# A two-layer decoder in one kernel: new instruction orders for all engines and one merged queue instead of three stages

## The chip, the cores and the metric

The kernel runs on one NeuronCore of one Trainium2 chip. The metric is the device time of one execution in microseconds. Before the change it is 4436.27 us, the median of 3 runs (4430.77 to 4455.68).

## The reference, cut to what matters

Input x is (64, 64, 128), that is 4096 tokens of width 128 in float32, with a context of the same shape. Six blocks follow one another, each with a residual and, outside it, a layernorm of its input:

```
x = x + delta_rule_attention(layernorm(x))          # "A": 4 heads, sequential rule over 64 tokens
x = x + causal_attention(layernorm(x), ctx)         # "B": 16 heads of 8
x = x + ffn_block(layernorm(x))                     # "C": 6 layers, each:
    #   y = local_attention(shift(y) @ Wqkv; 16 heads of 64, l2norm, rotary, window 32) @ Wo + y
    #   y = (a * gelu(gate)) @ W2 + y, with [a, gate] = layernorm(shift(y)) @ W1; 128 -> 2*341 -> 128
x = x + clipped_attention(layernorm(x))             # "D": 16 heads of 8
x = x + gated_attention(layernorm(x), ctx)          # "E": 8 heads of 16, exp and log gates
x = x + mixture_of_experts(layernorm(x))            # "F": 16 experts, top 3, all computed
```

All arithmetic is float32.

## The kernel before, in words

The 4096 tokens are 32 tiles of 128 tokens (two sequences of 64 each). x, y (the running value of block C) and the context stay in SBUF. Work is cut into units. A unit AB is blocks A and B of one tile (32 units). A unit C1 is the attention of one layer of block C for one tile (6 x 32 = 192), a unit C2 is the feed-forward part of one layer for a group of four tiles (6 x 8 = 48). A unit DE is blocks D, E and F of one tile (32 units). Units C1 and C2 stand in one sequence, in groups of five: four C1, then the C2 of an earlier group.

Each unit is a set of named phases on four engines ("pe", "act", "dve", "pool"); a phase is one to some hundred instructions and adds 1 to a semaphore of its unit when it ends. The order is written out by hand in the strings AB_ORDER, C_ORDER and DE_ORDER (lines 78 to 113). In such a string, `p04` says: in slot n, do phase p0 of unit n-4. The digit is the lag. In C_ORDER a 1 or 2 in front names C1 or C2. Slot after slot the whole string is walked, so each engine works on several units at once, in a fixed order; an engine that waits for a semaphore holds up everything behind it in its string. `program` (line 445) runs the three stages one after the other: all slots of AB, then a prelude, then all slots of C, then all slots of DE. On every engine the first phase of C stands behind the last phase of AB, and the first of DE behind the last of C. `all_ab` (line 299) makes the first users of BIG, the banks and the small tiles wait for the last eight AB units; `all_c` (line 303) does the same for DE.

PSUM has 8 banks (`bank`). AB and DE take them in turn (8), C takes 6 in turn and keeps banks 6 and 7 for the scores. BIG is a scratch area of 25,600 floats a partition, laid out anew for each stage by `ab_bufs`, `c_bufs`, `c2_bufs`, `de_bufs`. In C the arrays T1, T2 and sq are there twice (tiles t and t-2 share one), and qT, kT, VV and P three times.

A C1 unit goes: x (transpose in), q, k, v for halves 0 and 1 (matmul 128x512), squares on ScalarE, products with rotary tables on VectorE (lines with tile rc and rs), sums on GpSimd (q, k), norm by nine small VectorE steps n0 to n8, scaling on GpSimd (n0, n1, 128x1024), transposes a and b, scores s, maximum, exponential, row sum, reciprocal, scaling on GpSimd (p), transposes p, products y and w, output projection o. Line numbers in the profile are mostly those of helpers: L557 is a matmul, L561 a transpose, L901 a copy on ScalarE, L909 another activation, L1109 tensor_tensor, L1114 tensor_scalar, L1117 scalar_tensor_tensor and L1120 reduce on VectorE, L1549 tensor_tensor and L1552 inverse root on GpSimd.

In layer 0 of block C the layernorm of x makes y. It is made by `first_norm` and `first_pow` (tile mvF), which run in the orders as the phases `first` and `second`; they have semaphores of their own (rot0, rot1, y0) and are no phases of a unit.

In a DE unit the phase G makes the scores of E and the spread gates; then VectorE makes dm and mx, GpSimd d2, ScalarE ex (exponential), VectorE C, and PE ct (four transposes). Phases h and k are first expert layers (PE h, ScalarE relu h and k), o and x the second (PE o, VectorE x). ScalarE needs the functions Exp and Ln in each DE unit (g1 Exp, g2 Ln, x3, e0, e1, ex, em Exp) and Exp and Gelu in C.

## Time and profile before

| what | us |
|---|---|
| median of 3 runs | 4436.27 |
| span of the profiled execution | 4433.1 |
| PE busy (matmul) | 4137.5 (93%) |
| VectorE busy | 3566.6 (80%) |
| ScalarE busy | 3444.4 (78%) |
| GpSimd busy | 2650.6 (60%) |

The profiled execution is the span of 4433.1 us from its first instruction to its last; the median lies 3.2 us above it. The page cuts the span into 40 slices of 111 us. Block AB takes the first five slices, C the next 26, DE the rest. Busy time is the union of an engine's instructions; the end of a matmul is modelled. The granted clock is the TensorE clock as a share of full speed, 1.00 or 0.50 at any moment.

### The profile page before, as it was taken

The numbers are of one execution on the slowest core, as the hardware profiler recorded it, in microseconds if no ns is written. First come the engines' busy times: TensorE is split into PE (matmuls) and PEld (weight loads), VectorE is DVE, ScalarE is ACT, GpSimd is POOL, SyncE is SP. The second block draws the span as 40 slices with busy tenths as digits, with TensorE's granted clock in tenths as the row PEclk, the third lists the DMA queues.
The fourth block names the chain that finished last, engine by engine and source line by source line (L and its number), as shares of the span: only waits on it lengthen the run. The fifth ranks groups of instructions, "written<-read, shape, count | busy, mean of one in ns | idle before, by whom it ended". The sixth has DMA issues, their size and how long they took to land.

```text
span 4433.1 us, 150676 instructions
## 1 busy us (share of the span) xinstructions
PE 4137.5 (93%) x61520; PEld 3049.0 (69%) x61520; DVE 3566.6 (80%) x11101; ACT 3444.4 (78%) x9647; POOL 2650.6 (60%) x2210
## 2 busy tenths in 40 slices
PE   7999989999999999999999999999999689999999
PEld 5777756666666666666666666666666478888888
DVE  4666599999889888899898989898989357766775
ACT  3555478889888888888888988888888357776776
POOL 3444377777777777777777777777777133333331
PEclk8888899999999999999999999999999789999999
DMA  3000000000000000000000000000000100000000
GB/s 101 4 4 4 4 3 4 5 3 4 29 4 4 4 28 4 4 4 13 20 3 4 5 28 4 4 4 8 7 9 9 47 2 4 4 4 4 4 4 6
DMA packets 65258, 46.43 MB, mean 10 GB/s; under 512 B 29220, under 2 KB 63032, under 8 KB 63800
## 3 DMA queue, kind: packets, MB, share of 16 engines
q1 hardware_dynamic: 64568, 36.78, 2.9%
q8 instruction: 487, 7.98, 0.7%
q14 instruction: 203, 1.66, 0.1%
HBM read 28.48 MB, written 2.10 MB: 7 GB/s over the span
## 4 chain that ended last, share of the span: by engine, by line
PE 68%; ACT 13%; DVE 10%; POOL 5%; issue 5%; SPq 0%; DVEq 0%; DMA 0%; ACTq 0%; POOLq 0%
PE ps L557 56%; PE ps L561 12%; ACT BIG L909 7%; DVE BIG L1109 5%; POOL BIG L1549 5%; ACT L909 2%; ACT BIG L901 2%; DVE sm L1120 2%; ACT ps L901 1%; DVE BIG L1117 1%; DVE BIG L1114 1%; POOL sm L1552 0%; DVE sm L1117 0%; DVE BIG L1187 0%; DVE sm L1113 0%
## 5 line engine op out<-in xcount | busy, mean ns | idle before, releaser
L557 PE MATMUL ps<-WB,BIG 128*128 128x128 f32 (+2 forms) x8576 | 1941.9, 363 | 8.4 <-ACT BIG L901 3.4
L901 ACT ACTIVATE BIG<-ps 128x512 f32<-128x512 f32 (+6 forms) x3168 | 1484.0, 530 | 538.8 <-PE ps L561 407.7
L1549 POOL TENSOR_TENSOR BIG<-BIG,sm 128x512 f32<-128x512 f32 (+1 forms) x864 | 1219.0, 1426 | 788.7 <-DVE sm L1319 473.5
L557 PEld LDWEIGHTS ps<-WB,BIG 128*128 128x128 f32 (+1 forms) x8576 | 1142.2, 193 | 217.6 <-issue 175.6
L561 PEld LDWEIGHTS ps<-t_ident,BIG 128*128 128x128 f32 x6016 | 705.8, 144 | 541.4 <-issue 250.2
L561 PE MATMUL ps<-t_ident,BIG 128*128 128x128 f32 x6016 | 916.2, 282 | 162.5 <-ACT BIG L901 53.3
L1549 POOL TENSOR_TENSOR BIG<-BIG 128x512 f32<-128x512 f32 x768 | 967.2, 1280 | 144.1 <-DVE BIG L1109 144.1
L1120 DVE TENSOR_REDUCE sm<-BIG 128x8 f32<-128x512 f32 (+3 forms) x1472 | 882.6, 611 | 174.5 <-ACT BIG L909 172.2
L557 PEld LDWEIGHTS ps<-BIG 64*64 64x64 f32 (+2 forms) x37888 | 626.0, 130 | 364.6 <-issue 93.1
L557 PE MATMUL ps<-BIG 64*64 64x64 f32 (+4 forms) x37888 | 774.7, 225 | 69.7 <-ACT BIG L901 18.7
L909 ACT ACTIVATE BIG<-ps 128x512 f32<-128x512 f32 (+1 forms) x832 | 512.1, 616 | 257.3 <-PE ps L557 252.3
L909 ACT ACTIVATE BIG<-ps,sm 128x64 f32<-128x64 f32 (+1 forms) x3104 | 682.6, 360 | 20.3 <-DVE sm L1120 16.3
L557 PE MATMUL ps<-BIG,WB 128*128 128x128 f32 (+1 forms) x2624 | 568.5, 352 | 26.0 <-ACT BIG L909 26.0
L1552 POOL TENSOR_TENSOR sm<-sm,halfn 128x1 f32<-128x1 f32 (+2 forms) x336 | 293.8, 875 | 490.7 <-DVE sm L1113 335.8
L1109 DVE TENSOR_TENSOR BIG<-ps,rs 128x256 f32<-128x256 f32 x1536 | 570.7, 412 | 0.0
L1109 DVE TENSOR_TENSOR BIG<-ps,rc 128x512 f32<-128x512 f32 x768 | 524.2, 682 | 46.4 <-ACT BIG L909 40.5
L557 PEld LDWEIGHTS ps<-BIG,WB 128*128 128x128 f32 x2624 | 364.6, 191 | 188.6 <-issue 144.1
L909 ACT ACTIVATE BIG<-ps,t_F_b 128x128 f32<-128x128 f32 x1024 | 320.9, 379 | 46.8 <-PE ps L557 42.9
L1117 DVE SCALAR_TENSOR_TENSOR sm<-sm 128x32 f32<-128x32 f32 (+1 forms) x1216 | 283.2, 236 | 27.0 <-ACT sm L909 0.2
L1120 DVE TENSOR_REDUCE sm<-ps 128x8 f32<-128x512 f32 (+1 forms) x416 | 263.5, 643 | 29.9 <-PE ps L557 24.2
L901 ACT ACTIVATE ps<-t_bandm 128x512 f32<-128x512 f32 x384 | 231.1, 686 | 0.0
L909 ACT ACT_TABLE_LOAD x158 | 202.7, 1283 | 2.8
(120 smaller groups left out, 2985.1 us busy)
## 6 DMA issues: line engine op xcount, KB each, us to landing
WB<-in_Wqkv SPq DMA_DIRECT2D x6, 1536.0 KB, 7.4
XS<-y_sb SPq DMA_DIRECT2D x96, 63.0 KB
y_sb<-in_ctx SPq DMA_DIRECT2D x16, 256.0 KB, 3.1
WB<-in_Wo SPq DMA_DIRECT2D x6, 512.0 KB, 9.1
x_sb<-in_x SPq DMA_DIRECT2D x8, 256.0 KB, 5.0
WB<-in_F_W SPq DMA_DIRECT2D x1, 2048.0 KB, 8.6
WB<-in_F_W SPq DMA_DIRECT2D x8, 256.0 KB, 6.5
out<-x_sb SPq DMA_DIRECT2D x8, 256.0 KB, 2.3
```

What stands on the lines that cost most here:

```text
L557: return te.matmul(o, l, r, start=start, stop=stop, skip_group_check=not check)
L561: return te.transpose(o, i, ident[0:n, 0:n])
L901: return se.activation(o, i, ACT.Copy)
L909: return se.activation(o, i, f, **kw)
L1109: return ve.tensor_tensor(o, a, b, op)
L1114: return ve.tensor_scalar(o, a, s1, s2, op0, op1)
L1117: return ve.scalar_tensor_tensor(out=o, in0=a, scalar=s, in1=b, op0=op0, op1=op1)
L1120: return ve.tensor_reduce(o, a, AX, op, negate=negate)
L1549: return pe_.tensor_tensor(o, a, b, op)
L1552: return pe_.tensor_tensor(o, a, halfn[:, 0:n], ALU.pow)
```

## The change

All three order strings are new. In C the lags were 0 to 6 and are now 4 to 9 (the new norm phases 0 to 4); in AB and in DE they are 0 to 7 before and after. C has 12 rings of semaphores instead of 8. The three stages are no longer walked one after the other: `schedule(e)` gives each phase of each unit a due time, from a start and a slot length for each stage (BEGIN and SLOT, constants), sorts by it, and each engine works through the one merged list. So the last slots of AB and the first of C, and the last of C and the first of DE, are mixed. The slot lengths serve only for this sort. PSUM banks are given along the merged list of PE. The waits for a whole earlier stage (`all_ab`, `all_c`) are replaced by waits for the few phases whose buffers overlap (`after_one`, `after_two` and single waits). The norm of layer 0 becomes phases d1 to d4 (VectorE) and d (GpSimd) of the C1 units of layer 0. The rotary tables of layer l+1 are made at tile 30 of layer l rather than at tile 0 of layer l+1. The expert weights are loaded in two parts, the first while the last layer of C still runs. After the last Gelu ScalarE is told to load the table set `natural_log_exp_and_others`. New waits guard what the longer lags could overtake (the reduce phases wait for p0 and p1 of four tiles before, the mask b.M for the expert phases of two tiles before, x on ScalarE for q, k and v of four tiles before).

```diff
 C_ORDER = {
-    "pe": "2tr3 1v13 2a16 1k12 1p15 2o6 1o6 1b03 1a03 1q01 2g03 2g13 2g23 1b13 1a13 2a03 1v03 2a23 1p04 1q11 "
-          "1y5 1w5 1s3 1x0 1k01",
...
-    "pool": "1first1 1n13 1q12 1k02 1q02 1p04 1k12 2sh2 1p14 1n02",
+    "pe": "1w9 1s7 1x4 1p18 1k15 1p08 2a28 1v16 1o9 1a06 1q04 2a08 1b06 2o9 2g06 2g26 1b16 1a16 1q14 2g16 1v06 2a18 "
+          "1y8 2tr5 1k04",
+    "act": "1s18 1v17 1q05 1a07 1b07 1b17 2g07 1f07 1q15 2g27 1a17 1f17 2tr6 2sh5 2g17 1k05 1v07 1o09 1o19 1x4 1p18 "
+           "1k15 1p08 1s07",
...
+    "pool": "1k17 1d2 1n07 1n17 2sh6 1q06 1k06 1p08 1q16 1p18",
 }
...
+SLOT = {"ab": 13.5, "c": 11.5, "de": 25.2}
+BEGIN = {
+    "ab": {"pe": 4.7, "act": -27.6, "dve": -18.2, "pool": -15.0},
+    "c": {"pe": 420.5, "act": 404.6, "dve": 417.1, "pool": 398.8},
+    "de": {"pe": 3220.8, "act": 3178.2, "dve": 3200.7, "pool": 3210.1},
+}
...
 DE_ORDER = {
-    "pe": "om3 p12 oJ6 p02 av3 u2 hA5 oK6 t2 hO6 oL6 w2 hD5 hN6 oA5 gT5 hP6 oB5 b25 oC5 xc2 hG5 X11 hE5 oM6 g2 hF5 "
-          "oD5 J1 oP6 oN6 oO6 X34 oE5 hI5 hJ5 hH5 oF5 g34 cs2 oG5 hC4 hB4 T1 hK5 G2 s1 hM5 oI5 oH5 hL5 ct2",
+    "pe": "hL6 oH6 hA5 hD5 oI6 oJ6 ct3 p12 p02 hM6 om3 av3 u2 hN6 oK6 t2 X11 oL6 hO6 gT5 w2 J1 hP6 hE5 oA5 oM6 oB5 "
+          "b25 xc2 oN6 oO6 hG5 oC5 hF5 g2 oP6 oD5 oE5 oF5 X34 hI5 hH5 oG5 g34 cs2 hC4 hJ5 T1 hB4 hK5 G2 s1",
...
 AB_ORDER = {
-    "pe": "J1 b12 V3 s4 O3 a22 u5 b22 T1 o3 a32 w3 t5 G1 b32 D1 p14 a42 v4 x3 b42 X0 q3 Z2 y5 a11 W2 p04",
+    "pe": "b22 u5 a32 v4 o3 y6 T1 w3 b32 G1 D1 a42 p14 b42 x3 X0 t5 a11 Z2 b11 W2 q3 a21 V2 p04 J0 O2 s3",
...
+        def schedule(e):
+            due = []
+            for seq, order, stage in ((AB, AB_ORDER, "ab"), (CC, C_ORDER, "c"), (DE, DE_ORDER, "de")):
+                items = [(o[:-1], int(o[-1])) for o in order[e].split()]
+                for n in range(len(seq) + 10):
+                    for j, (ph, lag) in enumerate(items):
+                        u = unit(seq, n - lag)
...
+                        if u:
+                            due.append((BEGIN[stage][e] + SLOT[stage] * (n + j / len(items)), u, ph[1:] if stage == "c" else ph))
+            return [d[1:] for d in sorted(due, key=lambda d: d[0])]
...
-        def program(ab, c1, c2, de, name, before_c=(), tables=None):
...
+        def program(ab, c1, c2, de, name):
+            for u, ph in schedule(name):
+                {"AB": ab, "C1": c1, "C2": c2, "DE": de}[u.kind](u, ph)
...
+                    if u is last2 and ph == LAST_GELU:
+                        o.then_inc(u.name("act", ph, sems), 1)
+                        se.preload_act_table_set("natural_log_exp_and_others")
+                        return
...
+                        elif before(u, 4):
+                            w.wait_ge(*before(u, 4).on("pool", "p0"))
+                            w.wait_ge(*before(u, 4).on("pool", "p1"))
                         o = red(sm[:, 1, s8:s8 + 8], v64(b.sq), ALU.add)
...
+                    elif CC and ph == "xn1":
+                        before1 = uC1[(depth - 1, NT - 2 + min(t, 1))]
+                        w.wait_ge(*before1.on("pe", "a1"))
+                        w.wait_ge(*before1.on("pe", "b1"))
```

## Rows read from the trace of the kernel before

**Rows 1.** The page: busy digits in 40 slices, one digit a tenth.

```profile
PE   7999989999999999999999999999999689999999
PEld 5777756666666666666666666666666478888888
DVE  4666599999889888899898989898989357766775
ACT  3555478889888888888888988888888357776776
POOL 3444377777777777777777777777777133333331
PEclk8888899999999999999999999999999789999999
```

**Rows 2.** Windows 1000 to 3000 (C) and 3650 to 4350 (DE): busy us, instructions, clock.

```profile
core 0: us, PE busy (x) PEld busy (x) DVE busy (x) ACT busy (x) POOL busy (x), PEclk, DMA share, GB/s
1000.00:3000.00 2000.00, 1922.42 (x25333) 1312.51 (x25332) 1794.26 (x4852) 1779.15 (x4758) 1470.00 (x1099) 1.00 0.03 10
3650.00:4350.00 700.00, 645.89 (x7656) 593.92 (x7655) 488.17 (x2201) 494.76 (x1520) 225.85 (x280) 1.00 0.01 4
```

**Rows 3.** Tile XS, 1000 to 3000: one ScalarE copy a group; first and last start.

```profile
L901 ACT ACTIVATE XS<-y_sb x33: 442/443/445, 1021.9 to 2946.9; 128x256 f32<-128x256 f32 x33
```

**Rows 4.** Waits, 1000 to 3000: who waited for whom, us, times, longest.

```profile
POOL BIG L1549 <- DVE sm L1319: 321.7, 233, 4.1
PEld ps L557 <- issue: 233.1, 915, 2.1
PEld ps L561 <- issue: 159.1, 531, 2.5
ACT BIG L909 <- PE ps L557: 130.8, 235, 0.9
POOL BIG L1549 <- DVE sm L1117: 104.6, 34, 3.2
DVE y_sb L1109 <- PE ps L557: 53.5, 95, 3.8
DVE sm L1120 <- ACT BIG L909: 50.7, 66, 1.3
```

**Rows 5.** Chain that ended last, in order of time, in C: start, us, what.

```profile
2226.77 0.63 PE ps L561 x4
2227.40 1.79 PE ps L557 x16
2229.18 0.87 PE ps L561 x8
2230.06 0.86 PE ps L557 x2
...
2239.14 6.94 PE ps L557 x28
```

**Rows 6.** Windows of two neighbouring AB slots.

```profile
451.90:465.89 13.99, 13.52 (x476) 10.60 (x477) 9.97 (x40) 7.79 (x30) 7.13 (x8) 1.00 0.02 4
465.89:482.59 16.70, 16.24 (x477) 12.46 (x478) 10.05 (x40) 8.11 (x30) 7.17 (x8) 0.80 0.02 4
```

**Rows 7.** Windows around the change from AB to C.

```profile
500.00:550.00 50.00, 41.58 (x843) 33.47 (x843) 21.50 (x71) 18.79 (x56) 12.84 (x16) 0.75 0.01 2
550.00:600.00 50.00, 36.44 (x236) 18.50 (x235) 45.35 (x119) 28.73 (x81) 34.06 (x28) 0.84 0.01 3
600.00:650.00 50.00, 45.71 (x697) 30.84 (x697) 49.11 (x134) 44.12 (x124) 41.27 (x34) 1.00 0.01 2
```

**Rows 8.** Chain in the first C slots: start, us, what.

```profile
594.35 0.51 POOL sm L1552
594.86 7.79 POOL BIG L1549 x6
602.65 2.30 issue
604.98 2.90 POOL BIG L1549 x2
607.89 0.51 POOL sm L1552
```

**Rows 9.** Windows around the change from C to DE.

```profile
3450.00:3500.00 50.00, 29.63 (x259) 18.29 (x257) 16.66 (x50) 13.37 (x27) 3.91 (x5) 0.77 0.35 98
3500.00:3550.00 50.00, 31.22 (x272) 22.77 (x276) 17.57 (x74) 16.29 (x41) 10.32 (x14) 0.53 0.02 5
3550.00:3600.00 50.00, 37.59 (x358) 30.80 (x350) 24.39 (x105) 19.87 (x52) 15.77 (x19) 0.60 0.00 1
```

**Rows 10.** Chain in DE, one slot and the start of the next.

```profile
3632.71 0.88 ACT BIG L909 x3
3633.61 1.28 ACT L909
3635.49 0.71 PE ps L557 x4
...
3659.89 0.88 ACT BIG L909 x3
```

**Rows 11.** Waits in DE, 3600 to 4350: us, times, longest.

```profile
PEld ps L561 <- DVE BIG L1117: 38.9, 28, 1.4
PE ps L557 <- ACT BIG L909: 24.6, 28, 0.9
```

**Rows 12.** Groups of instructions on ScalarE, 3620 to 4433, table loads.

```profile
L909 ACT ACT_TABLE_LOAD x56 | 71.8, 1283 | 1.0
```

**Rows 13.** Tile out: stores of the result, eight groups of four tiles.

```profile
L541 SPq DMA_DIRECT2D out<-x_sb x8: 372/372/388, 3713.1 to 4430.3; - x8
```

More of the change, by code:

```diff
@@ L107 @@
 C_ORDER = {
[7 rows of a table removed]
[7 rows of a table added]
 }
-SILENT = ("first", "second")
+NORM = ("d1", "d2", "d3", "d", "d4")
 for _kind in "12":
@@ L160, in __init__ @@
         self.base = dict(base)
-        self.marks = MARKS["C2f" if at.get("last") else kind]
+        self.marks = MARKS[kind + "f" if at.get("last") or at.get("l") == 0 and kind == "C1" else kind]
         self.count = dict.fromkeys(ENG, 0)
@@ L399, in c_phases @@
-        def c_phases(e, n):
-            for o in C_ORDER[e].split():
-                u = unit(CC, n - int(o[-1]))
-                if u and u.kind == "C" + o[0]:
-                    yield u, o[1:-1]
-        full, turn = [None] * 6, 0
-        for u in CC:
+        def schedule(e):
[5 more added lines that the diff above has]
+                        u = unit(seq, n - lag)
+                        if u and stage == "c" and (u.kind[1] != ph[0] or ph[1:] in NORM and u.at["l"]):
+                            continue
+                        if u:
+                            due.append((BEGIN[stage][e] + SLOT[stage] * (n + j / len(items)), u, ph[1:] if stage == "c" else ph))
+            return [d[1:] for d in sorted(due, key=lambda d: d[0])]
@@ L408, in build, with take @@
+        full, turn, primed = [()] * 8, 0, [(), ()]
+        for u in AB + CC + DE:
             if u:
                 u.bank, u.after = {}, {}
-        for n in range(SLOTS_C if CC else 0):
-            for u, ph in c_phases("pe", n):
-                if u.kind == "C1" and ph in "sw":
-                    u.bank.update({"s0": 6, "s1": 7} if ph == "s" else {})
-                    u.after[ph] = ()
-                    continue
-                if u.kind == "C1" and ph == "y":
-                    u.after[ph] = []
-                    for h in "01":
-                        u.bank["y" + h] = turn % 6
-                        u.after[ph] += full[turn % 6] or []
-                        full[turn % 6] = [(u, "act", "o" + h)]
-                        turn += 1
-                    continue
-                u.bank[ph], u.after[ph] = turn % 6, full[turn % 6]
-                full[turn % 6] = [(u, *m.split()) for m in EMPTIED[u.kind[1] + ph]]
-                turn += 1
+        def take(u, ph, marks, wide, banks):
+            nonlocal turn
+            turn += turn % wide
+            u.bank[ph], u.after[ph] = turn % banks, ()
+            for i in range(wide):
+                u.after[ph] += full[(turn + i) % banks]
+                full[(turn + i) % banks] = tuple((u, *m.split()) for m in marks)
+            turn += wide
@@ new lines, in build @@
+        order = schedule("pe")
+        places = [i for i, (u, ph) in enumerate(order) if u.stage == "c"]
+        for i, (u, ph) in enumerate(order):
+            banks = 6 if places and places[0] <= i <= places[-1] else 8
+            if places and i == places[0]:
+                primed = [full[6], full[7]]
+            u.after[ph] = ()
+            if u.stage == "ab":
+                if ph in AB_EMPTIED:
+                    take(u, ph, AB_EMPTIED[ph], 1 + (ph in AB_PAIRS), banks)
+            elif u.stage == "de":
+                if ph in DE_EMPTIED:
+                    take(u, ph, DE_EMPTIED[ph], 1 + (ph in DE_PAIRS), banks)
+            elif u.kind == "C1" and ph == "s":
+                u.bank.update({"s0": 6, "s1": 7})
+                full[6], full[7] = ((u, "act", "s0"),), ((u, "act", "s1"),)
+            elif u.kind == "C1" and ph == "y":
+                for h in "01":
+                    take(u, "y" + h, ("act o" + h,), 1, 6)
+                u.after["y"] = u.after["y0"] + u.after["y1"]
+            elif u.kind == "C2" or ph != "w":
+                take(u, ph, EMPTIED[u.kind[1] + ph], 1, 6)
@@ L690, in pe_bank @@
             def pe_bank(u, ph):
[L692 to L695 removed]
+                for v, e, m in u.after[ph]:
                     w.wait_ge(*v.on(e, m))
@@ L701, in half, with prime @@
                 return slice(64 * (par ^ hf), 64 * (par ^ hf) + 64)
+            def prime(h):
+                w.wait_ge("k_a", 16 * len(SETS["a"]))
+                for v, e, m in primed[h]:
+                    w.wait_ge(*v.on(e, m))
+                for i in range(4):
+                    o = mm(bank[6 + h][:, 128 * i:128 * i + 128], ident[:, :], ident[:, :], start=(i == 0), stop=(i == 3))
+                o.then_inc(sems["prime"], 1)
             def pe_c1(u, ph):
```

206 lines of the change are left out of this document (96 added, 110 removed), and 28 rows, old and new, of tables (AB_ORDER, C_ORDER, DE_ORDER).

## The prediction

> **What bounds the kernel now.** I read the page's digits first [rows 1]: PE stands at 9 of 10 nearly throughout, with a dip where AB gives way to C (slice 5) and a deeper one where C gives way to DE (slice 31), and the granted clock is below 1.0 in AB and in both dips. So there are five places to look at: three steady stages and two hand-overs. Each stage is then read by its period and by what PE does in it.
>
> Block C: 33 copies into XS, one a group, start 1021.9 to 2946.9, so a group (four C1, one C2) takes 1925 / 32 = 60.16 us [rows 3]. PE is busy 1922.42 of 2000 us there [rows 2], or 57.83 us a group; VectorE by the same rule 53.97, ScalarE 53.52, GpSimd 44.2. Three engines are thus between 89 and 96%, and what is left to win is PE's idle 2.33 us a group. Is a busy PE really at work? In the chain the pieces of PE stand against each other with no gap (1.79 us from 2227.40, 0.87 from 2229.18, 0.86 from 2230.06), and one piece of 28 matmuls takes 6.94 us [rows 5]. So I take 57.83 as PE's own load.
>
> Block AB: two neighbouring slots take 13.99 and 16.70 us with 476 and 477 matmuls [rows 6]; the first at clock 1.00, with PE busy 13.52, the second at clock 0.80. Mean 15.35. PE's load at the full clock is 13.5.
>
> Block DE: the same piece of ScalarE stands in the chain at 3632.71 and 3659.89, so a slot takes 27.18 us [rows 10]. PE is busy 645.89 of 700 [rows 2], 25.08 a slot; 2.10 us are idle. Two waits make them: the four transposes ct wait up to 1.4 us for C of VectorE, 38.9 us in 28 slots, and PE waits for a relu (24.6 in 28) [rows 11], which in the chain stands directly behind a table load of 1.28 us [rows 10].
>
> PE's load with no idle time would be 32 x 13.5 + 48 x 57.83 + 32 x 25.08 = 4010 us, against a span of 4433.1. The change removes no matmul, so all it can win lies in these 423 us.
>
> **The change, part by part.** The profiled span is 4433.1; the median of the runs is 3.2 higher, and I add that at the end.
>
> (1) C in steady state. The lags grow by about three slots, so a phase finds its inputs ready even if its neighbour is late. PE's idle 2.33 us a group has two bounds: nothing goes (60.16) or all of it goes (57.83). In the waits of C [rows 4] PE's own queue shows mostly "issue" and each single wait of the others is 1 to 4 us long, the kind that more distance covers; but VectorE and ScalarE, at 53.97 and 53.52 us, would be at 93% of a 57.83 us group, in a fixed order, so that each late phase is passed on. I take 0.7 us left: 58.5 a group. Gain 1.65 x 47 = 78 us (bounds 0 and 110).
>
> (2) AB in steady state. At the full clock PE idles 0.47 us a slot; the halved clock costs 16.70 - 13.99 = 2.7 us in every second slot, 1.35 a slot [rows 6]. The order is new and it puts the scores s between O and u, the phases with very small matmuls, which before stood almost together (O3 a22 u5). Whether the clock then stays up no row tells: bounds are 15.35 (as now) and 13.5. I take the middle, 14.3. Gain 32 x 1.05 = 34 us (bounds 0 and 59).
>
> (3) Hand-over from AB to C. PE idles 8.4, 13.6 and 4.3 us in the three windows from 500 to 650 [rows 7], 26 us, where C's own rate of idling would be 6; and at clocks 0.75 and 0.84 at most 12.5 + 8 us of full-speed time are lost. First C slots cost 13.6 us on GpSimd (its inverse root at 594.35 and 607.89, with 2.30 us of waiting between [rows 8]), since it has nothing of AB to do meanwhile. In the merged list AB's last phases fill this. Upper bound 41, lower bound 0; I take 27.
>
> (4) DE in steady state. Each slot now has two table loads: 56 in the last 813 us, or 30 slots, at 1283 ns [rows 12]. They come because Exp and Ln alternate. With a set that holds both in place they need not come again: 2.6 us less on ScalarE a slot, which itself is not the bound (494.76 of 700 busy [rows 2], 19.2 a slot). What counts is the relu behind the load, 0.9 us of PE a slot [rows 11]. The ct of a unit moves from four phases behind G and s to six behind, into the next slot; each h or o phase is four matmul instructions of this size, and eight took 0.87 us [rows 5], so 0.44 a phase and 0.9 us more cover for a wait of 1.4. So 2.1 - 0.9 - 0.9 = 0.3 us stay: 25.4 a slot. Gain 1.78 x 29 = 52 us (bounds 0 and 61). The last three slots drain in any case.
> The row shows 1283 ns a load. The Trainium skill (ScalarE: Activation LUTs, section on table sets) lists natural_log_exp_and_others as holding exp and ln, one load for both, and gives about 2.7 us a load; by that price ScalarE would win 5.4 us a slot, but as it is not the bound the sum would be the same.
>
> (5) Hand-over from C to DE. From 3450 to 3600 PE idles 20.4, 18.8 and 12.4 us, and the clock is at 0.77, 0.53 and 0.60 [rows 9]. Idle beyond C's rate: 46 us; what the low clock costs on top is up to 55 us at a PE always busy, less at the 98 us it was busy: some 36. Upper bound 82 in all, lower bound 0. DE units can't start much earlier, though: xn1 of tile 0 waits for the transposes of the last but one C1 unit, xn2 for the projection of the last, and a DE unit is a chain over six slots before its experts feed PE. And the longer lags of C make its tail longer: the last C2 ends nine slots after its number, not six. I take 35.
>
> (6) Added waits. The norm phases are the same instructions as before. The reduce phases wait for GpSimd's p of four tiles before: behind them on VectorE stand i and the next slot's norm and q, and who waits is PE's transposes. By the diff's constants that p is 17.7 us ahead; if it weren't, 0 to 1.3 us a tile (the longest such VectorE wait in C is 1.3 for ScalarE [rows 4]), 0 to 250 in all; I take 0 here and keep the upper end in R5. The wait of e0 is for a phase that stands earlier in VectorE's own string. The expert weights start earlier and hide under C.
>
> Sum: 78 + 34 + 27 + 52 + 35 = 226. 4433.1 - 226 = 4207, and 3 for the median: 4210 us.
>
> **A second way to the same number.** The diff's own constants are slots of 13.5, 11.5 (57.5 a group) and 25.2, within 1% of PE's loads above, so they are a pace with PE never idle. At that pace tile 3 would leave its last expert at 3200.7 + 25.2 x (3 + 7.36) = 3462, against the first store at 3713.1, and the last at 4430.3 [rows 13], 717 later; 28 slots at 2.0 less make 661. That ends at 4124. My slots add 47 x 1.0 in C, 32 x 0.8 in AB and 6 in DE: 4203. The two ways differ by 4 us.
>
> **The rivals.**
> R1, C stays at its period. T1, T2 and sq are still there only twice. A unit's half 0 is written by VectorE at lag 4, place 34 of 38, and read by PE at lag 6, place 13 of 25; with PE's begin 3.4 us later that is 1.9 slots of the 2 there are, leaving about 1 us. If this loop, and not the distance, sets the 60.16, gain (1) is gone: 4288. For it: VectorE and ScalarE waits in C are spread over many small rows [rows 4], as in a closed loop. Against: PE idles only 4%.
> R2, the clock in AB stays as it is: half the slots at 16.7, gain (2) is only the idle 0.2: 4210 + 28 = 4238, inside my own range.
> R3, the plan's pace is met: 4124 + 3 = 4127.
> R4, PE isn't the bound. Weight loads on PE are busy 1312.51 of 2000 us [rows 2], 39.5 a group, so if matmul time could still shrink, VectorE would be next with 53.97 and its own small gaps, about 55: 3.5 x 47 = 165 more, 4045. Against it stand rows 5, where pieces follow without a gap and yet take their full time. The Trainium skill (Trainium Kernel Development and Optimization, Performance Expectations) says that busy matmul time is a bad measure and that of the weight loads is a good one; by that rule this rival would hold.
> R5, slower: GpSimd becomes the bound. Its queue waits for n8 of VectorE (104.6 us in 34 waits of up to 3.2 us [rows 4]) with q, k and p of other units behind it. In the first slots of C such a queue made each slot 13.6 us [rows 8]. If the new order (k1, d, n0, n1, then q0, k0, p0, q1, p1) holds that for all five slots of a group, a group takes 68 us: 7.84 x 47 = 368 more than now against 148 gained elsewhere, 4433 + 3 + 220 = 4656. It decides from 60.16 + 148 / 47 = 63.3 us a group on. Against: GpSimd has 44.2 us of work in a group, and its waits before were idle time it could spare.
> R6, the overlap gives nothing or costs as much as it brings, since two stages share six banks: 4433 + 3, no change, with the steady gains lost to late banks as well.
>
> **How the numbers follow.** Forecast, with R2 in it (4150 to 4265): 0.60. R1, 4288 and around it: 0.20. R3: 0.07. R4: 0.03. R5: 0.07. R6: 0.03. The predicted time is the likeliest case, 4210. The range takes in R1 with half of the hand-overs lost (4340) and R3 (4130): what is left out is R4, R5, R6 and the edges, under 0.2. A measurement of this kernel can tell about 0.5% from no change. Faster by more: 0.90; within 0.5%: 0.03; slower: 0.07.
>
> **What would show it.** In the profile after: copies into XS 58.5 us apart (60.2 under R1, 55 under R4, over 63 under R5); AB slots of 13.5 without, or 15 to 16 with, a halved clock; no table load after the last Gelu; DE slots of 25.4 and no 1.4 us wait of a transpose for C of VectorE; PE digits of 8 or more in both hand-overs. PE's busy time should fall from 4137 towards 4050, by the clock only. If PE's idle time is not smaller in all five places, the forecast's reasons are wrong even where its number holds.

## The result, and the profile after

The changed kernel takes 4617.94 us (median of 4 runs, 4600.22 to 4627.52), the kernel before 4440.59 us beside it on the same chip (4 runs too): a ratio of 1.0386, 95% interval 1.0361 to 1.0412. It is slower by 4%, where I had forecast 5% less time. The profiled execution of after spans 4598.3 us against 4433.1 us, 165.2 us more; the accounts below are made between these two.

The page of after: busy time of each engine, busy tenths in 40 slices of 115 us, granted clock, and below it the engines of the chain that ended last.

```profile
PE 4218.3 (92%) x61520; PEld 3077.7 (67%) x61520; DVE 4009.8 (87%) x11101; ACT 3384.6 (74%) x9586; POOL 2644.3 (58%) x2210
...
PE   7999989999999999999999999999999889999999
...
DVE  4666599999999999999999999999999767777776
...
PEclk9989899999999999999999999999999989999999
...
DVE 44%; PE 43%; issue 7%; POOL 3%; ACT 3%; SPq 0%; DMA 0%; POOLq 0%; DVEq 0%; ACTq 0%
```

Against [rows 1] the second dip is shallower (8 instead of 6), as forecast, but VectorE's digits in C went from 8 and 9 to 9 throughout. It is busy 443 us longer in all (3566.6 before) and carries 44% of the chain (10% before). The windows of C and of DE, and then the one copy a group of C:

```profile
1000.00:3000.00 2000.00, 1861.60 (x24135) 1241.74 (x24134) 1959.37 (x4583) 1694.67 (x4505) 1389.84 (x1042) 0.99 0.03 9
3850.00:4350.00 500.00, 471.00 (x5371) 438.39 (x5370) 361.32 (x1534) 295.74 (x1015) 155.09 (x196) 0.95 0.02 4
```
```profile
L907 ACT ACTIVATE XS<-y_sb x32: 413/416/420, 1011.9 to 2982.8; 128x256 f32<-128x256 f32 x32
```

The group of C takes 1970.9 / 31 = 63.58 us instead of 60.16 [rows 3]. VectorE is busy 1959 of 2000 us (1794 before [rows 2]), TensorE 1862 (1922 before): VectorE is the bound.

To cut each trace into the same five stretches I use three instructions of VectorE whose records are complete in the whole traces: the masked product `BIG<-ps,t_upd` (once a tile in AB, 32), the adds into y_sb out of PSUM (C, 240, first and last) and the experts' adds into x_sb (DE, 512). Before, then after (columns: shortest/median/longest ns, first to last start us; the y_sb line up to 900 us):

```profile
L1109 DVE TENSOR_TENSOR BIG<-ps,t_upd x32: 423/425/426, 20.0 to 499.9; 128x256 f32<-128x256 f32 x32
...
L1109 DVE TENSOR_TENSOR y_sb<-y_sb,ps x24: 271/288/677, 611.0 to 897.6; 128x128 f32<-128x128 f32 x20, 128x512 f32<-128x512 f32 x4
...
L1117 DVE SCALAR_TENSOR_TENSOR x_sb<-ps,BIG,x_sb x512: 329/347/354, 3598.1 to 4429.9; 128x128 f32<-128x128 f32 x171
```
```profile
L1126 DVE TENSOR_TENSOR BIG<-ps,t_upd x32: 400/411/425, 20.2 to 537.9; 128x256 f32<-128x256 f32 x32
...
L1126 DVE TENSOR_TENSOR y_sb<-y_sb,ps x20: 273/274/675, 641.1 to 889.2; 128x128 f32<-128x128 f32 x17, 128x512 f32<-128x512 f32 x3
...
L1134 DVE SCALAR_TENSOR_TENSOR x_sb<-ps,BIG,x_sb x512: 328/345/353, 3750.1 to 4594.6; 128x128 f32<-128x128 f32 x171
```

The last y_sb add starts at 3484.0 before and 3716.0 after. That gives the table in which all kernels of this study are read (us; the "slot" is the first stretch over 31):

| kernel | AB, 31 slots (slot) | AB to C | C, first to last add (group) | C to DE | DE's experts |
|---|---|---|---|---|---|
| before | 479.9 (15.48) | 111.1 | 2873.0 (60.16) | 114.1 | 831.8 |
| after | 517.7 (16.70) | 103.2 | 3074.9 (63.58) | 34.1 | 844.5 |
| difference | +37.8 | -7.9 | +201.9 | -80.0 | +12.7 |

With 0.7 us at the two ends the differences make the 165.2 us.

**Where C's time went.** VectorE has no new work in C. Its small steps, n0 to n8 of each tile (128x32, the norm with its inverse root) and the add of eps for a C2 (`ep`), take longer. Before, then after, over the same 2000 us (columns: count, busy us, mean ns, idle before):

```profile
L1117 DVE SCALAR_TENSOR_TENSOR sm<-sm 128x32 f32<-128x32 f32 x665 | 167.8, 252 | 17.8
...
L1109 DVE TENSOR_TENSOR sm<-sm 128x32 f32<-128x32 f32 x399 | 76.6, 192 | 13.6
...
L1117 DVE SCALAR_TENSOR_TENSOR sm<-sm,magic 128x32 uint32<-128x32 uint32 x133 | 24.1, 181 | 1.1
```
```profile
L1134 DVE SCALAR_TENSOR_TENSOR sm<-sm 128x32 f32<-128x32 f32 x626 | 222.7, 356 | 2.2
...
L1126 DVE TENSOR_TENSOR sm<-sm 128x32 f32<-128x32 f32 x376 | 217.5, 579 | 5.4
...
L1134 DVE SCALAR_TENSOR_TENSOR sm<-sm,magic 128x32 uint32<-128x32 uint32 x125 | 96.3, 770 | 1.1
...
L1130 DVE TENSOR_SCALAR sm<-mv 128x4 f32<-128x4 f32 x32 | 34.6, 1083 | 0.0
```

`ep` took 5.6 us in 33 before. So the small steps cost 274.1 us of 2000 before, 8.24 us a group, and 571.1 us after, 18.15 a group: 9.9 us more, on an engine that had 6.2 to spare. One of them in the timeline of after, VectorE and then GpSimd (start, us):

```profile
2209.90 1.16 DVE L1126 TENSOR_TENSOR sm<-sm 128x32 f32<-128x32 f32 x1
```
```profile
2209.74 1.27 POOL L1587 TENSOR_TENSOR BIG<-BIG 128x512 f32<-128x512 f32 x1
```

The step starts while GpSimd's instruction runs and ends with it, at 2211.06 against 2211.01. The same operation takes 0.192 us otherwise (the median in both kernels). The timelines of the two engines, laid over each other from 1000 to 3000 us, show it for every one of these tensor_tensor steps: in after 157 of the 376 start while a GpSimd instruction runs, take 0.96 to 1.21 us and end 45 to 54 ns behind it; the 219 others fall into pauses of GpSimd and take 0.17 to 0.19 us. In before all 399 fall into pauses. Reduces, reciprocals and everything that reads PSUM last the same in both kernels (the reduce 128x512 669 and 672 ns). The Trainium skill (SBUF — State Buffer, section Who interferes with whom) gives a reason: VectorE's second port pair is GpSimd's too, held by one of them at a time, and a VectorE instruction with two SBUF inputs, or a tensor_scalar in its faster mode, needs it, a reduce never; "Issue order, not op shape, decides who blocks." No trace shows the ports, but the lengths agree: 0.19 and up to 1.2 us for one and the same instruction, and the 94 scalar_tensor_tensor steps that GpSimd's instruction joins only after their start keep their 0.19 us. In before's strings n4 to n7 stood side by side, as did n1 and n2; in after's they stand one by one between long phases.

### The profile page after: what moved, and what is told of

It reads as the page before. It is cut to its first block, busy times and chain, and to the rows that moved or that the text cites. A ratio compares the mean times of both kernels' runs of the same rounds, so it can differ in the third digit from the quotient of the medians.

```text
span 4598.3 us, 150804 instructions
## 1 busy us (share of the span) xinstructions
PE 4218.3 (92%) x61520; PEld 3077.7 (67%) x61520; DVE 4009.8 (87%) x11101; ACT 3384.6 (74%) x9586; POOL 2644.3 (58%) x2210
## 4 chain that ended last, share of the span: by engine, by line
DVE 44%; PE 43%; issue 7%; POOL 3%; ACT 3%; SPq 0%; DMA 0%; POOLq 0%; DVEq 0%; ACTq 0%
PE ps L564 37%; DVE BIG L1126 14%; DVE sm L1137 11%; PE ps L568 7%; DVE sm L1126 6%; DVE sm L1134 5%; POOL BIG L1587 3%; DVE BIG L1134 2%; DVE BIG L1131 2%; ACT BIG L915 1%; ACT BIG L907 1%; DVE y_sb L1131 1%; DVE y_sb L1126 1%; DVE BIG L1130 1%; DVE sm L1338 1%
## 5 line engine op out<-in xcount | busy, mean ns | idle before, releaser
L564 PE MATMUL ps<-WB,BIG 128*128 128x128 f32 (+2 forms) x8576 | 1974.1, 368 | 75.0 <-DVE BIG L1126 36.6
L907 ACT ACTIVATE BIG<-ps 128x512 f32<-128x512 f32 (+5 forms) x3168 | 1452.8, 507 | 560.8 <-PE ps L568 479.1
L568 PE MATMUL ps<-t_ident,BIG 128*128 128x128 f32 x6016 | 898.9, 281 | 146.4 <-POOL BIG L1587 71.1
L1137 DVE TENSOR_REDUCE sm<-BIG 128x8 f32<-128x512 f32 (+3 forms) x1472 | 898.7, 613 | 76.6 <-ACT BIG L915 74.2
L564 PE MATMUL ps<-BIG 64*64 64x64 f32 (+3 forms) x37888 | 790.2, 226 | 130.6 <-DVE BIG L1126 92.4
L564 PE MATMUL ps<-BIG,WB 128*128 128x128 f32 (+2 forms) x2624 | 599.7, 357 | 11.5 <-ACT BIG L915 11.5
L564 PEld LDWEIGHTS ps<-BIG,WB 128*128 128x128 f32 (+1 forms) x2624 | 370.4, 195 | 184.1 <-issue 116.5
L1134 DVE SCALAR_TENSOR_TENSOR sm<-sm 128x32 f32<-128x32 f32 (+1 forms) x1216 | 373.6, 309 | 8.7 <-ACT sm L915 0.8
L1126 DVE TENSOR_TENSOR sm<-sm 128x32 f32<-128x32 f32 (+1 forms) x736 | 356.3, 484 | 13.2
L907 ACT ACTIVATE ps<-t_bandm 128x512 f32<-128x512 f32 x384 | 250.2, 652 | 0.0
```

Of the source, the lines that this page charges most:

```text
L564: return te.matmul(o, l, r, start=start, stop=stop, skip_group_check=not check)
L568: return te.transpose(o, i, ident[0:n, 0:n])
L907: return se.activation(o, i, ACT.Copy)
L1126: return ve.tensor_tensor(o, a, b, op)
L1134: return ve.scalar_tensor_tensor(out=o, in0=a, scalar=s, in1=b, op0=op0, op1=op1)
L1137: return ve.tensor_reduce(o, a, AX, op, negate=negate)
```

## The experiments

Theory S: these stretched steps make VectorE the bound of C. Rival L: the longer lags through buffers that are there only twice do. Group and whole time tell.

**1. The steps back together.**

```diff
-    "dve": "1d10 1n66 1q15 1n76 2a19 1r15 1n86 1l05 ... 1n05 1d41 1o9 1n15 2ep5 1u07 1n25 2a28 ...
+    "dve": "1d10 1n16 1n26 1n36 1n46 1n56 1n66 1n76 1n86 1q15 2a19 1r15 1l05 ... 1n05 1d41 1o9 2ep5 1u07 2a28 ...
```

> The kernel after with one edit: in C's VectorE string the steps n1 to n8 stand together, at the place of n8, and no longer one by one over a slot. Theory S (small VectorE steps that read two operands from SBUF last as long as the GpSimd instruction that runs beside them; 18.2 us a group against 8.2 before): GpSimd waits for n8 at that time, so the steps run beside an idle GpSimd; they fall to below 10 us a group, the group from 63.6 to 58 to 60 us, the kernel to 4340 to 4430 us. Rival L (the longer lags over buffers that are there twice close a loop and set 63.6): the group stays at 63 to 64, the kernel within 1% of 4618.

Measured: 4744.44 us, ratio 1.0655 (1.0634 to 1.0675), group 66.46. Expectation missed. The steps got shorter only to 15.4 us a group, and GpSimd waits longer for n8, 260.6 us in 120 waits (205.8 in 94 in after); VectorE is busy 1845 of 2000 us, and TensorE 1835. Half of the tensor_tensor steps, 180 of 360, still start while a GpSimd instruction runs and take 0.92 to 1.21 us:

```profile
L1126 DVE TENSOR_TENSOR sm<-sm 128x32 f32<-128x32 f32 x360 | 235.7, 655 | 12.3
```

A run of neighbours is no protection where it does not fall into a pause of GpSimd. That a chain of eight dependent steps at one place delays GpSimd's n0 and n1 (the scaling) is my reading of the longer waits. So this run does not tell S from L.

**2. Steps that cannot be stretched.** A reciprocal has one SBUF input. In C n0 to n8 become nine reciprocals of the same 128x32; the inverse root isn't computed in this kernel.

```diff
-                        o = newton(u, sm[:, 5, 0:32], sm[:, 2, 0:32], sm[:, 6, 0:32], i - 1)
+                        t_ = sm[:, 6, 0:32]
+                        o = ve.reciprocal(*((t_, sm[:, 2, 0:32]) if i % 2 else (sm[:, 5, 0:32], t_)))
```

> The kernel after with the same order and the same count, but in C the steps n0 to n8 are reciprocals of 128x32 with one SBUF operand (the inverse root is not computed). Theory S: each such step stays near 0.2 us whatever GpSimd does; about 10 us a group leave VectorE and the group falls from 63.6 to 57.8 to 60 us. Rival L: order, lags and buffers are unchanged, so the group stays at 63 to 64 us.

Measured: 4423.58 us, ratio 0.9940 (0.9920 to 0.9959), group 59.37.

```profile
1000.00:3000.00 2000.00, 1965.05 (x25725) 1322.85 (x25724) 1898.26 (x4914) 1786.22 (x4824) 1485.47 (x1115) 1.00 0.03 10
```
```profile
L1300 DVE RECIPROCAL sm<-sm 128x32 f32<-128x32 f32 x1077 | 367.3, 341 | 9.3
```
```profile
L907 ACT ACTIVATE XS<-y_sb x34: 594/597/603, 1007.8 to 2967.0; 128x256 f32<-128x256 f32 x34
```

All of them last 0.30 to 0.36 us, whatever GpSimd does, not the 0.2 us that I had expected; the group lies in theory S's range all the same. The small steps take 13.2 us a group instead of 18.15, and with the lags and buffers of after TensorE gets to 1965 of 2000 us. L falls.

**3 and 4. The other way round.** In the kernel before the small steps alternate with long phases (run 3), or are made reciprocals too (run 4).

```diff
-    "dve": "1first0 1n42 1n52 1n62 1n72 1i14 1n82 2a23 1r01 1q11 1s03 ... 1u13 1n01 1q00 1n11 1n21 2tr1 1n31 ...
+    "dve": "1first0 1n42 1i14 1n52 2a23 1n62 1r01 1n72 1q11 1n82 1s03 ... 1n01 1u13 1n11 1q00 1n21 2tr1 1n31 ...
```

> The kernel before with one edit: n1 to n8 alternate with other phases in VectorE's string, at lags as before. Theory S: the small steps meet GpSimd's instructions more often; their mean of 0.24 us rises and the group grows by 1 to 4 us, the kernel to 4480 to 4620. Rival L: lags and buffers are those of before, within 0.5% of 4440.

Measured: 4585.28 us, ratio 1.0303 (1.0269 to 1.0337), group 62.73, as theory S expected. Spreading the steps and nothing else makes before nearly as slow as after; they rise from 8.24 to 12.8 us a group.

```profile
L1109 DVE TENSOR_TENSOR sm<-sm 128x32 f32<-128x32 f32 x383 | 103.7, 271 | 6.6
...
L1117 DVE SCALAR_TENSOR_TENSOR sm<-sm,magic 128x32 uint32<-128x32 uint32 x128 | 91.9, 718 | 1.1
```

> The kernel before with its order, and the steps n0 to n8 of C as reciprocals with one SBUF operand (the inverse root is not computed). It is the control of the run on the kernel after. Theory S: before, these steps cost 252 and 192 ns a piece, little above their bare time, so at most 1.5 us a group are to be had: 4370 to 4440. If it gains as much as the run on the kernel after (over 3 us a group), the reciprocals themselves are cheaper and that run tells nothing of GpSimd.

Measured: 4556.98 us, ratio 1.0239 (1.0219 to 1.0260), group 62.18. The expectation of 4370 to 4440 us was missed: in before the reciprocals cost more than the steps that they replace (12.75 us a group against 8.24), so they make that kernel slower, and what run 2 gains does not come from the reciprocals being cheaper than the unstretched steps.

```profile
L901 ACT ACTIVATE XS<-y_sb x32: 442/446/447, 1051.3 to 2979.0; 128x256 f32<-128x256 f32 x32
```

Runs 2 and 4 have the same small steps at a fixed cost (13.2 and 12.75 us a group), so their groups compare the orders of C alone: 59.37 against 62.18. With VectorE's work this long the new orders are worth 2.8 us a group. Against before itself (60.16) run 2 is only 0.8 us shorter.

**5 and 6. The steps off VectorE.** The inverse root as two ScalarE activations, z1 (Ln) and z2 (Exp); only n0 stays. One table set holds Ln and Exp and is loaded behind the last Gelu of each group, so that the loads stay at two a group. Run 5 on after, run 6 on before (there `1z13` and `1z23`).

```diff
-    "act": "... 2sh5 2g17 1k05 1v07 1o09 ...
+    "act": "... 2sh5 2g17 1z16 1k05 1z26 1v07 1o09 ...
+                if ph[0] == "z":
+                    w.wait_ge(*(u.on("dve", "n0") if ph == "z1" else u.on("act", "z1")))
+                    o = act(sm[:, 6, 0:32], sm[:, 2, 0:32], ACT.Ln) if ph == "z1" else act(sm[:, 5, 0:32], sm[:, 6, 0:32], ACT.Exp, scale=-0.5)
...
-                    w.wait_ge(*u.on("dve", "n8"))
+                    w.wait_ge(*u.on("act", "z2"))
```

> The kernel after, with stage C's eight VectorE steps n1 to n8 (inverse roots of the norms, 128x32) replaced by two ScalarE activations a tile, z1 = Ln and z2 = Exp(-0.5 x), and the table set that holds both loaded after the third Gelu of every group; only n0 stays on VectorE. The result is the same function. Theory S (after is slow because GpSimd stretches VectorE's small two-operand steps, so that VectorE becomes the bound): with the steps gone VectorE's small work falls from 18.15 us a group to about 5, VectorE from 1959 to about 1700 us of 2000, TensorE stands near 1970 of 2000, the group takes 58.0 to 59.0 us instead of 63.6, and the whole 4350 to 4400 us (the variant with reciprocals took 59.4 and 4424, with 13 us of small steps left). The rival L (the longer lags through two-deep buffers set the 63.6 us, whatever the small steps last): the group stays over 62 us, the whole over 4550. Rival A (the chain VectorE to ScalarE to GpSimd waits behind ScalarE's queue, 2 more activations a tile and Exp after Ln): group 60 to 61, the whole 4450 to 4500.

> The kernel before with the same replacement: n1 to n8 of stage C as two ScalarE activations, with before's orders. Theory S: VectorE is not the bound in the kernel before (1794 us of 2000), and its steps there were short already, so that little is to be had: group 59.3 to 60.3 us instead of 60.16, the whole 4380 to 4450. That bounds from the other side what the new orders are worth once the contention is out of the way: after with Ln and Exp less before with Ln and Exp, expected 30 to 80 us in favour of the new orders. Rival O (the new orders of stage C are worth nothing even then, and all of a gain comes from Ln and Exp): both kernels with Ln and Exp within 15 us of each other.

Measured: run 5 4440.7 us, ratio 0.9990 (0.9970 to 1.0010), group 60.23; run 6 4659.79 us, ratio 1.0492 (1.0457 to 1.0526), group 64.92. Run 5's windows and chain:

```profile
1000.00:3000.00 2000.00, 1945.03 (x25389) 1306.24 (x25389) 1646.02 (x3784) 1804.14 (x5017) 1459.73 (x1094) 1.00 0.03 10
```
```profile
PE 51%; ACT 29%; DVE 15%; issue 4%; POOL 1%; SPq 0%; DMA 0%; ACTq 0%; DVEq 0%; POOLq 0%
```

VectorE is at 82%, its share of the chain fell from 44 to 15%, and after loses its whole deficit of 177 us: S holds for where the time went. Its forecast of 4350 to 4400 us and 58 to 59 us a group was missed: the group is 60.2, in rival A's range, and ScalarE's share of the chain rose from 3 to 29%. That ScalarE is what keeps the group from 58.5 was not tested by itself. Run 6's expectation was missed by 210 us. ScalarE stands still for n0 at each z1, which has not come yet at its place in before's short lags:

```profile
L909 ACT ACTIVATE sm<-sm 128x32 f32<-128x32 f32 x246 | 55.4, 225 | 204.4 <-DVE sm L1127 203.5
```

203.5 us in 2000, 6.6 a group: a misplaced phase, so that run 6 says nothing of what the new orders of C are worth; runs 2 and 4 stand for it. For DE it is a clean case, though. Its strings there are before's, and with the table set loaded behind the last Gelu no table is loaded in DE. Before, then run 6:

```profile
3850.00:4350.00 500.00, 460.49 (x5479) 423.27 (x5478) 348.56 (x1569) 353.25 (x1084) 162.70 (x201) 1.00 0.01 4
```
```profile
3850.00:4350.00 500.00, 482.49 (x5446) 447.38 (x5445) 344.94 (x1563) 305.66 (x1040) 160.13 (x199) 0.95 0.01 4
```

ScalarE is busy 48 us less and TensorE idles 22 us less, but for about as many matmuls TensorE is busy 22 us longer, at a granted clock of 0.95 instead of 1.00, and the experts take 832.9 us against 831.8: no gain.

**7. The stages one after another.**

```diff
-    "c": {"pe": 420.5, "act": 404.6, "dve": 417.1, "pool": 398.8},
-    "de": {"pe": 3220.8, "act": 3178.2, "dve": 3200.7, "pool": 3210.1},
+    "c": {"pe": 620.5, "act": 604.6, "dve": 617.1, "pool": 598.8},
+    "de": {"pe": 3720.8, "act": 3678.2, "dve": 3700.7, "pool": 3710.1},
```

> The kernel after with the stages one after another: the begin times of C put 200 us and those of DE 500 us later, so that no phase of C is queued ahead of one of AB, nor one of DE ahead of one of C; every order within a stage is as it was. The trace says that the stretch from the last add of C to the end of the span became 67 us shorter, and I put that to the overlap of C and DE: theory M says that this is lost, and 0 to 30 us at AB to C, 4618 + 67 to 97 = 4685 to 4715. The rival (the overlap takes place, but costs in C what it gives in DE, since VectorE is the bound there): under 4650. The group period in the middle of C should stay 63.6 by both.

Measured: 4667.57 us, ratio 1.0502 (1.0468 to 1.0536), between the two forecasts. By stretches: AB 541.0 (slot 17.45), AB to C 118.9, C 3036.9 (group 63.59), C to DE 100.1, experts 854.4. Against after the overlap of AB and C is worth 15.7 us (the merged stretch is 103.2 us in after, and 102.8 to 108.4 in runs 8, 9 and 12). That of C and DE gives 66.0 us and takes 38.0 back in C's last slots, where DE's phases now stand in between: 28 net. The rest of the 77 us between the spans is AB's slot and DE's, whose strings are the same in both; they differ from run to run with the clock (0.91 and 0.84 from 100 to 500 us).

**8. Without the table load behind the last Gelu.**

```diff
-                        se.preload_act_table_set("natural_log_exp_and_others")
```

> The kernel after without its one load of the natural_log_exp table set behind the last Gelu: DE's Ln and Exp then load their sets in turn, some 62 loads of 1.283 us more, 158 instead of 97. By the theory that ScalarE has time in DE (353 us busy of 500 before, 296 after) the time rises by 0 to 20 us, to 4618 to 4638. By the rival that each load stands on the way (as I had let it in the upper bound of my DE term) it rises by up to 80 us, to 4700, with a slot of 28 to 29 us instead of 26.6.

Measured: 4613.35 us, ratio 1.0392 (1.0367 to 1.0418): no difference to after; the rival's 80 us did not come. The loads come back, 160 of 1.283 us instead of 98 (before: 159, with [rows 12]'s 56 in DE). DE's experts take 833.8 us, less than after's 844.5. Its window stands against that of after above:

```profile
3850.00:4350.00 500.00, 462.23 (x5403) 428.61 (x5404) 369.33 (x1550) 340.17 (x1064) 158.87 (x199) 0.98 0.02 4
```

TensorE is busy 9 us less in 500 and yet does a little more. The granted clock is 0.98 against 0.95: run 6's finding, the other way round.

**9. Two stretched phases moved,** in AB `xn2` away from the start of GpSimd's l, in DE `rg` behind C.

```diff
-    "dve": "m3 e3 st0 xn25 q3 t03 ag0 d44 ...
+    "dve": "m3 e3 st0 q3 t03 ag0 xn25 d44 ...
...
-"... ag10 dm3 mx3 c12 su5 rc5 c02 rg5 C3 mm3 ...
+"... ag10 dm3 mx3 c12 su5 rc5 c02 C3 rg5 mm3 ...
```

> The kernel after with two phases of VectorE's strings moved, no operation changed: in AB the norm xn2 (128x128 tensor_scalar, 0.34 us alone and 1.23 us beside GpSimd's l) three phases later, from right behind e3, whose end starts l, to behind ag0; in DE rg5 (128x16, 1.18 us beside GpSimd's d2) from ahead of C3 to behind it. Theory S says that either stretch stands on the way of its slot: AB's slot falls from 15.8 us by 0.4 to 0.9, so that C's first add comes 13 to 29 us earlier than 641.1 us, and DE's slot falls from 26.6 by 0.5 to 0.9, 15 to 28 us in all; the whole 4560 to 4590 us instead of 4618. The rival (these two stretches fill time in which TensorE's string would have waited for something else): 4605 to 4625, first add at 636 to 645, DE's slot at 26.6.

Measured: 4600.37 us, ratio 1.0340 (1.0315 to 1.0365). AB's slot stays, 16.74. The whole misses both ranges. In DE `rg` falls from 1.26 to 0.22 us, the transposes ct wait 14.0 us for C instead of 24.8, and the experts take 834.4 us instead of 844.5:

```profile
PEld ps L564 <- ACT BIG L915: 15.5, 18, 0.9
PEld ps L564 <- DVE BIG L1134: 14.0, 19, 0.8
```

Confirmed in DE: the experts take 844.5 to 859.4 us in the seven traces that have after's DE strings and its table load, 834.4 here and 837.7 in run 11, so some 7 to 25 us of the 15 to 28. The rival holds in AB.

**10. The old strings of AB.** All four strings of AB from before, AB ahead of C, the rest as after.

```diff
 AB_ORDER = {
-    "pe": "b22 u5 a32 v4 o3 y6 T1 w3 b32 G1 D1 a42 p14 b42 x3 X0 t5 a11 Z2 b11 W2 q3 a21 V2 p04 J0 O2 s3",
+    "pe": "J1 b12 V3 s4 O3 a22 u5 b22 T1 o3 a32 w3 t5 G1 b32 D1 p14 a42 v4 x3 b42 X0 q3 Z2 y5 a11 W2 p04",
...
-    "ab": {"pe": 4.7, "act": -27.6, "dve": -18.2, "pool": -15.0},
+    "ab": {"pe": -9e3, "act": -9e3, "dve": -9e3, "pool": -9e3},
```

> The kernel after with stage AB's strings of the kernel before on all four engines, run to their end ahead of C (begin of AB far below that of C); C, DE and their overlap as in after. By the addition of stretches (theory M: the overlap of AB and C gives nothing, since the unmerged variant had C's first add 39 us later and its last add at the same time, 3717 against 3716; and the new AB strings cost 30 us against the old ones) C's first add comes at 611 as in the kernel before, the stretch of C takes 3037 as in the unmerged variant, the rest 882: 4530 us. The rival (AB's strings are neutral, the later first add comes from the way into C, the layer-0 norms as phases included): first add at 640 to 680, the whole 4560 to 4600.

Measured: 4590.47 us, ratio 1.0315 (1.0286 to 1.0344). AB's slot is 15.64, C's first add comes at 625.0 us, so the strings are worth 1.06 us a slot, 33 us, and 17 of them go again with the overlap (AB to C 120.3); the medians say 27 us less than after. The whole lies in the rival's range, the first add in neither. My 4530 was wrong by a false addition: I had put the 38 us by which C was shorter in run 7 to its head. Here C takes 3076.0 us with its head unmerged and its end merged, so they belong to the end.

**11. Everything at once:** run 5, the AB strings of run 10 and `rg` behind C.

> The kernel after with everything at once that the runs point to: AB's strings of the kernel before, unmerged from C; C's inverse roots as Ln and Exp on ScalarE; in DE rg5 behind C3; the overlap of C and DE kept. By addition of stretches: first add 611, C 2902 less up to 38 (unmerged at its head), the rest 891 less up to 27: 4340 to 4404 us, ratio to the kernel before 0.976 to 0.991. The rival (gains at one place are given back at the next, as the overlap of AB and C was): the same as the kernel after with Ln and Exp alone, 4441.

Measured: 4394.07 us, ratio to before 0.9878 (0.9852 to 0.9905), as forecast by addition: 1.2% less than before and faster than both kernels. Its busy times and windows:

```profile
PE 4207.9 (96%) x61520; PEld 3093.3 (70%) x61520; DVE 3381.2 (77%) x9565; ACT 3394.6 (77%) x9970; POOL 2642.0 (60%) x2210
```
```profile
1000.00:3000.00 2000.00, 1945.78 (x25421) 1307.25 (x25417) 1649.61 (x3784) 1800.97 (x5023) 1462.99 (x1097) 1.00 0.03 10
```

Stretches: AB 489.1 (15.78), AB to C 111.2, C 2898.2 (60.15), C to DE 33.8, experts 837.7. It keeps the gain at the second hand-over (80 us against before); elsewhere it is slower than before by 9 us in AB, 25 in C (the group is 60.15 against 60.16, so it lies at C's ends) and 6 in DE.

**12. xn2 ahead of l.** Run 9 could not tell for AB, since xn2 moved by as much as it was stretched.

```diff
-    "dve": "m3 e3 st0 xn25 q3 ...
+    "dve": "m3 xn25 e3 st0 q3 ...
```

> The kernel after with one phase of AB's string on VectorE moved: xn2 from right behind e3 and st0 to right ahead of e3, whose end starts GpSimd's l. xn2 then runs before l (0.34 us instead of 1.23) and is not started later, since its input pw2 ends at the moment it starts now (220.52 against 220.56 us); VectorE may stand 0.3 us for it. In the trace of after TensorE's x waits 25 us for xn2 in 400. Theory X (the 0.9 us by which xn2 is stretched stands on the way of AB's slot; moving it three phases back, as the run before did, gave its end the same place, and so could show nothing): AB's slot, read from the K multiplications, falls from 16.70 by 0.6 to 0.9 us, C's first add comes 19 to 28 us earlier than 641, the whole 4590 to 4600 instead of 4618. The rival (the loop is the new string's own: norm, x, q, s and the two softmax halves one behind the other within a slot): the slot stays at 16.4 to 16.8, the first add at 635 to 647.

Measured: 4627.72 us, ratio 1.0416 (1.0392 to 1.0440), slot 16.89, first add at 652.1 us: theory X is missed, and both values lie just above the rival's. xn2 now takes 0.34 us each time, and the chain goes over e and GpSimd's l behind it instead. Pieces of the chain, start and us:

```profile
204.74 0.57 POOL sm L1590
205.59 0.29 DVE BIG L1126
205.96 1.28 POOL BIG L1587
207.37 0.65 PE ps L564 x33
```

So in AB the stretch is not what costs. In every kernel with the new AB strings (eight traces) the slot is 16.7 to 17.5 us, and 15.5 to 16.0 with the old ones. Which phase of the new strings does it was not found.

## Why the prediction was wrong, point by point

The sum gave 4207 us for the span; it is 4598.3. The misses of the five terms add up to the 391 us:

| term | forecast | measured | miss |
|---|---|---|---|
| 1, group of C, 47 times | -78 | +161 (63.58 - 60.16) | 239 |
| 2, slot of AB | -34 | +38 | 72 |
| 3, AB to C | -27 | -8 | 19 |
| 4, DE | -52 | +13 | 65 |
| 5, C to DE, with C's tail | -35 | -39 (201.9 - 161 - 80.0) | -4 |

**Term 1** failed at the sentence that VectorE would stand at 93% of a group with 53.97 us of work. I carried an engine's load from the old order into the new as if an instruction's length were its own. It became 62.3 us (1959.37 x 63.58 / 2000), more than before's whole group. The sign was in the trace of before, had I asked for spreads and not for means: the same 128x32 step lasts 192 ns in the median and 900 at most. (Columns: shortest/median/longest.)

```profile
L1117 DVE SCALAR_TENSOR_TENSOR sm<-sm x665: 177/192/900, 1007.2 to 2995.5; 128x32 f32<-128x32 f32 x167
```

The part on distance is borne out in part only: at equal and long small steps the new orders win 2.8 us a group (runs 2 and 4), but against before's 60.16 the shortest group is run 2's 59.37, 0.8 us of my 1.65, and with the steps on ScalarE it is 60.2 (runs 5 and 11). TensorE's own load was right: 57.8 to 58.7 us a group in before and in runs 2 to 5 and 11 (59.2 in after), and no group came below it. So the rival R4, that a busy TensorE is no bound, is not borne out: in run 5 VectorE has 18% to spare, ScalarE 10% and TensorE 3%, and the group is 60.2 us, TensorE's busy 58.6 and little more. The Trainium skill (Trainium Kernel Development and Optimization, Performance Expectations) calls matmul busy time a bad measure of how close a kernel is to its limit, by which the group could have fallen further; no run here shows it.

**R1** (the double buffers) fell with run 2, whose group is below 60.16 with the same buffers. (The last VectorE write of half 0 in the new string is `1r04`, place 35 of 36 and not 34 of 38; by my own sum that leaves 1.8 us and not 1.) **R2** was right on the clock in AB, not on its slot. **R3** fell with term 1, and **R6** with run 7, in which both overlaps prove to be worth something (15.7 and 28 us). **R5** named GpSimd as the cause of a slower kernel, and put the turning point at 63.3 us a group. The group is 63.58 and GpSimd is the cause, but as the neighbour whose instructions stretch VectorE's, not as the bound: it works 44.2 us a group as before, and its waits for n8 doubled.

```profile
POOL BIG L1587 <- DVE sm L1134: 205.8, 94, 4.9
```

That line was 104.6 in 34 [rows 4]. It is the consequence: VectorE is late with n8. TensorE's busy time, which should have fallen from 4137 towards 4050 us, rose to 4218.3.

**Term 2.** My bounds were 15.35 and 13.5 a slot, with no loss among them, though the order of all four strings was new and I had followed none of its waits. (The old lags of AB went up to 8, in GpSimd's `u08`, not 7.) The slot became 16.70, at a clock of 0.91, no lower than before (0.89). TensorE idles 1.4 us a slot instead of 0.5 and waits above all for xn2, for the 25.1 us of the last line (windows before, after, and the wait of after):

```profile
100.00:500.00 400.00, 388.01 (x12412) 300.58 (x12411) 260.19 (x986) 206.47 (x729) 185.33 (x181) 0.89 0.02 4
```
```profile
100.00:500.00 400.00, 367.60 (x11581) 284.87 (x11578) 261.86 (x928) 197.84 (x677) 172.49 (x173) 0.91 0.02 4
```
```profile
PEld ps L568 <- DVE BIG L1131: 25.1, 24, 1.2
```

Run 12 shows that the stretch of xn2 is not the cause: without it the slot stays. That the old strings bring 15.64 back (run 10) puts the 1.06 us to the new strings; through which phase stays open.

**Term 3.** The overlap itself is worth 15.7 us (run 7); the new strings alone would have lengthened this stretch by 7.8.

**Term 4.** No table is loaded after the last Gelu but the one, as forecast, and ScalarE has 58 us more time in 500 (353 busy before). It was worth nothing (runs 6 and 8). ct still waits for C, 1.5 us at most, as GpSimd's d2 stretches the `rg` in front of it (run 9); the 0.9 us of cover that I gave it were priced from eight transposes [rows 5], not from h and o phases. And one term was missing, the clock. Per slot (28.03 us after, 27.28 before, from 17 gaps of the add `x_sb<-x_sb,ps`) TensorE's idle time did fall, from 2.16 to 1.63 us, but its busy time for the same matmuls rose from 25.12 to 26.40, with the granted clock at 0.95 instead of 1.00. In run 9 the idle time is 0.98 and the busy time 26.63 at 0.94; in run 8, with the loads back, 2.08 and 25.50 at 0.98. What the denser order gives is taken back by a lower clock, and 25.12 us of full-speed work at 0.95, 0.94 and 0.98 would be 26.4, 26.7 and 25.6. Run 6 shows the same with before's strings. My own slot before, 27.18, was one slot of the chain, and fair.

**Term 5** was right in size, though made differently: 80 us at the hand-over itself, near the upper bound, less what DE's phases cost C's end.

## What to carry to other kernels

Before an order is changed, list for each engine the instructions whose longest time is several times their median, and look at what runs beside them. In these traces small VectorE steps with two SBUF inputs, and most tensor_scalars from SBUF, last until the GpSimd instruction that was already running has ended (0.19 us became up to 1.21, 0.34 up to 1.99), so their cost belongs to the order and not to the instruction: keep them in GpSimd's pauses, give them one SBUF input, or put them on ScalarE. Cost a new order of four strings with a loss among its bounds, and take hand-overs, steady stages and tails apart by markers that each trace has; here, of the five terms, only the hand-over from C to DE brought a gain that lasted.
